# A conditioned ternary FFN on one core: c made three token groups ahead, in halves between the products of w1 and w3

## What is computed

```python
q_emb = relu(cond @ W3 + b3)                       # 128 x 256
v_sum = sum(x, axis=1, keepdims=True)              # x is 128 x 32 x 256
c = relu(((32 * x + v_sum) * q_emb[:, None, :]) @ W2 + b2)
w1q, w3q, w2q = ternary_quant(w1), ternary_quant(w3), ternary_quant(w2)
h1, h3 = c @ w1q.T, c @ w3q.T                      # 682 hidden columns
out = x + (silu(h1) * h3) @ w2q.T
# ternary_quant(w): s = mean(|w|); clip(round(w / s), -1, 1) * s
```

## Time and profile before

| | us |
|---|---|
| median of 3 runs | 182.1 |
| lowest and highest | 181.93, 182.63 |
| span of the profiled execution | 180.4 |
| PE busy in the span | 169.6 |
| DVE busy | 117.4 |
| ACT busy | 86.0 |
| POOL busy | 35.2 |

### The profile page before, as it was taken

The page is one execution under the profiler, slowest core; times in us unless marked ns, Lnnn a source line. Parts: engine busy times, 40 slices in busy tenths (PEclk is TensorE's granted clock), DMA queues, the critical chain, the costliest instruction groups (busy, mean ns, idle before and its releaser), DMA issues.

```text
span 180.4 us, 2908 instructions
## 1 busy us (share of the span) xinstructions
PE 169.6 (94%) x958; PEld 147.0 (81%) x958; DVE 117.4 (65%) x171; ACT 86.0 (48%) x142; POOL 35.2 (20%) x32
## 2 busy tenths in 40 slices
PE   6999899997379999999999999999999999999993
PEld 6788788885257898888889888888888988988893
DVE  0558999899993735674485565549357456744873
ACT  3135358857048744345463543555435443553640
POOL 4261677695925000000000000000000000000000
PEclk9999999999979999999999999999999999999999
DMA  4799734899000000030020003003000200300203
GB/s 94 244 336 360 231 116 124 280 359 290 0 0 5 0 0 0 0 116 0 0 90 26 0 0 116 0 0 116 0 0 19 97 0 0 116 0 0 89 31 116
DMA packets 14989, 15.21 MB, mean 84 GB/s; under 512 B 560, under 2 KB 14728, under 8 KB 14984
## 3 DMA queue, kind: packets, MB, share of 16 engines
q1 hardware_dynamic: 14976, 15.14, 25.7%
q10 hardware_dynamic: 8, 0.00, 0.0%
HBM read 10.94 MB, written 4.19 MB: 84 GB/s over the span
## 4 chain that ended last, share of the span: by engine, by line
PE 80%; DVE 10%; DMA 3%; issue 2%; ACT 2%; POOL 1%; SPq 0%; DVEq 0%; POOLq 0%
PE bank L482 46%; PE bank L512 23%; DVE w_t L607 5%; PE bank L403 5%; DMA w_sb<-in_L_ffn_w_dram 3%; DVE below L600 2%; PE bank L390 2%; PE bank L419 2%; DVE vsum L574 1%; POOL x L266 1%; ACT w_t L332 1%; PE bank L468 1%; PE bank L431 1%; ACT c_hi L318 1%; DVE y L579 0%
## 5 line engine op out<-in xcount | busy, mean ns | idle before, releaser
L482 PE MATMUL bank<-c_hi,T 128*128 (+3 forms) x176 | 69.9, 397 | 0.0
L482 PE MATMUL bank<-c_lo,T 128*128 (+3 forms) x176 | 69.7, 396 | 0.0
L355 ACT ACTIVATE y<-bank,checked 128x512 f32<-128x512 f32 (+1 forms) x48 | 33.0, 688 | 58.8 <-PE bank L482 58.8
L482 PEld LDWEIGHTS bank<-c_lo,T 128*128 128x128 f32 (+1 forms) x176 | 33.4, 190 | 6.2
L482 PEld LDWEIGHTS bank<-c_hi,T 128*128 128x128 f32 (+1 forms) x176 | 33.4, 190 | 6.2
L669 DVE TENSOR_TENSOR y<-y,bank 128x512 f32<-128x512 f32 x32 | 22.0, 686 | 22.1 <-PE bank L482 18.5
L512 PE MATMUL bank<-T,g_lo 128*128 128x256 f32 x160 | 32.7, 283 | 0.0
L512 PE MATMUL bank<-T,g_hi 128*128 128x256 f32 x160 | 32.5, 282 | 0.0
L403 PE MATMUL bank<-x,W_sb 128*128 128x256 f32 x128 | 29.9, 384 | 0.9 <-POOL x L266 0.9
L512 PEld LDWEIGHTS bank<-T,g_hi 128*128 128x128 f32 x160 | 27.1, 190 | 2.4
L669 DVE TENSOR_TENSOR x<-y,bank 128x512 f32<-128x512 f32 (+1 forms) x16 | 11.0, 688 | 26.5 <-ACT y L355 16.0
(11 more groups left out here) (61 smaller groups left out, 101.0 us busy)
## 6 DMA issues: line engine op xcount, KB each, us to landing
xo<-in_x_dram SPq DMA_DIRECT2D x1, 4096.0 KB, 16.9
out_dram<-xo SPq DMA_DIRECT2D x15, 256.0 KB, 2.2
xs<-in_x_dram SPq DMA_DIRECT2D x7, 512.0 KB, 3.9
w_sb<-in_L_ffn_w_dram SPq DMA_DIRECT2D x2, 640.0 KB
w_sb<-in_L_ffn_w_dram SPq DMA_DIRECT2D x1, 682.0 KB, 8.3
xs<-in_x_dram SPq DMA_DIRECT2D x2, 256.0 KB, 3.4
W_sb<-in_L_cond_W_dram SPq DMA_DIRECT2D x1, 256.0 KB, 5.2
out_dram<-xo SPq DMA_DIRECT2D x2, 128.0 KB, 2.0
```

The source lines that it names most:

```text
L355: nc.scalar.activation(silu[j % 2][r], h1[j % 3][r], ACT.Silu, scale=checked[r, 0:1]).then_inc(silu_done, 1)
L482: last = pe.matmul(dst[j % 3][0:w, :], T13[:, k, col:col + w], part[:, at(g), k, :], start=(i == 0), stop=(i == len(passes) - 1))
```

## The change

Only three groups (`AHEAD`), six halves, of c are made ahead. Half n of the other ten is made during the steps of the group three before its own: `half_at` places the transposes of its two halves behind the products of steps 0 and 2, and its multiplications by W2 behind those of steps 2 and 5. A half is now the unit of every engine's work on c: `relu(n)` is two ACT instructions of 256 columns, `hi_of_c` and `lo_of_c` one of 512, and `lo_of_c` is always POOL's. `ct` has four half buffers.

x is loaded once, straight into `xo`, from where PE transposes it; DMAs of x wait for nothing, and cond and W3 are loaded from ACT's queue. The rest rows of w1 and w3 are zeroed, so each of |w|'s sum, `below` and `w_t` is one instruction of 1536 columns, and all three sums of |w| are ACT's. `below` is formed with two operations, times -1 and greater than the limit, so `neg_limits` is gone. DVE instead of ACT copies w3's part of T13.

The h1 and h3 banks are two pairs in place of three; the banks set free hold `xT` (bank 6) and `z` (bank 7) during the layer. DVE does g and lo of the same step one behind the other. The group loops are written out.

```diff
-        h1 = [bank[:, 2 * s, :] for s in range(3)]
-        h3 = [bank[:, 2 * s + 1, :] for s in range(3)]
-        o = [bank[:, 6 + b, :].rearrange("p (t d) -> p t d", t=2) for b in range(TT // 2)]
...
+        h1 = [bank[:, 2 * s, :] for s in range(2)]
+        h3 = [bank[:, 2 * s + 1, :] for s in range(2)]
+        o = [bank[:, 4 + b, :].rearrange("p (t d) -> p t d", t=2) for b in range(TT // 2)]
+        o_last = bank[:, 6, 0:D]
...
+            g, j = m // STEPS, m % STEPS
+            return (g + AHEAD) * HALVES + at.index(j) if g + AHEAD < NG and j in at else None
...
+            for n in range(2):
+                sp.dma_start(xo[:, 1, n * HTT:(n + 1) * HTT], x_v[1, :, n * HTT:(n + 1) * HTT]
+                             ).then_inc(got_half[2 + n], 16)
+            sp.wait_ge(zeroed, 2)
+            sp.dma_start(w1_sb[:, 0:HC, :], w1[0:HC * P, :].rearrange("(j p) d -> p j d", p=P)).then_inc(got_w1, 16)
+            sp.dma_start(w1_sb[0:HR, HC, :], w1[HC * P:H, :]).then_inc(got_w1, 16)
+            sp.dma_start(xo[:, 2], x_v[2]).then_inc(got_group[0], 16)
+            sp.dma_start(w3_sb[:, 0:HC, :], w3[0:HC * P, :].rearrange("(j p) d -> p j d", p=P)).then_inc(got_w3, 16)
+            sp.dma_start(w3_sb[0:HR, HC, :], w3[HC * P:H, :]).then_inc(got_w3, 16)
             sp.dma_start(w2_sb[:], w2.rearrange("(c p) h -> p c h", p=P)).then_inc(got_w2, 16)
-            with sp.Fori(1, NG // 2 - 1) as i:
-                for u in range(2):
-                    sp.wait_ge(xT_done, (i * 2 + u + 1) * HALVES)
-                    sp.dma_start(xs[u][:], x_v[bass.ds(i * 2 + u + 2, 1)].rearrange("a p t d -> p (a t) d")
-                                 ).then_inc(got_xs[u], 16)
-            sp.dma_start(xo[:], x_v.rearrange("g p t d -> p g t d")).then_inc(got_xo, 16)
-            with sp.Fori(0, NG - 1) as g:
+            for g in range(3, NG):
+                sp.dma_start(xo[:, g], x_v[g]).then_inc(got_group[g - 2], 16)
...
+            scale_by_q(0)
+            scale_by_q(1)
+            for n in range(2, NH):
+                scale_by_q(n)
+                lo_of_c(n - 2)
+            lo_of_c(NH - 2)
+            lo_of_c(NH - 1)
...
+            relu(0)
+            hi_of_c(0)
+            abs_sum(0, w1_sb, w1_t, got_w1, 32)
+            relu(1)
+            hi_of_c(1)
+            relu(2)
+            hi_of_c(2)
+            abs_sum(1, w3_sb, w3_t, got_w3, 32)
+            relu(3)
+            hi_of_c(3)
+            abs_sum(2, w2_sb, w2_t, got_w2, 16)
+            relu(4)
+            hi_of_c(4)
+            copy_T13(0, T1_copied)
+            relu(5)
+            hi_of_c(5)
...
+            for m in range(NG * STEPS):
+                silu_step(m)
+                n = half_at(m - 1, (2, 5)) if m else None
+                if n is not None:
+                    relu(n)
+                hi_step(m)
+                if n is not None:
+                    hi_of_c(n)
+                if m == 0:
...
+            transpose_x(2)
+            project_c(0)
+            transpose_x(3)
+            project_c(1)
...
+            sum_partitions(0)
+            transpose_x(4)
+            project_c(2)
+            transpose_x(5)
+            project_c(3)
+            sum_partitions(1)
+            project_c(4)
+            transpose_w13(0, w1_t)
+            project_c(5)
+            transpose_w13(1, w3_t)
+            pe.wait_ge(T1_copied, 2)
+            sum_partitions(2)
...
-                pe.wait_ge(g_lo_done, g * STEPS + j + 1)
+            def h1_step(m):
+                j = m % STEPS
+                if j == 0:
+                    pe.wait_ge(c_lo_done, HALVES * (m // STEPS + 1))
+                if m >= 2:
+                    pe.wait_ge(g_done, m - 1)
+                hidden_product(m, h1, (j if j < HC else 2 * HC) * P, h1_done)
+            def h3_step(m):
+                hidden_product(m, h3, (HC + m % STEPS) * P, h3_done)
...
+            pe.wait_ge(y_done, EARLY)
+            pe.wait_ge(relu_done, DC * EARLY)
+            h1_step(0)
+            pe.wait_ge(limit_done, 3)
+            h1_step(1)
+            pe.wait_ge(T3_copied, 2)
+            h3_step(0)
+            transpose_w2()
+            h3_step(1)
+            LAST = (NG - 1) * STEPS
+            for m in range(NG * STEPS):
+                j = m % STEPS
+                if m >= 2:
+                    h1_step(m)
+                    if j < HC:
+                        h3_step(m)
+                n = half_at(m, (0, 2))
+                if n is not None:
+                    transpose_x(n)
+                n = half_at(m, (2, 5))
+                if n is not None:
+                    project_c(n)
+                ready = m - 2
+                if 0 <= ready < LAST and ready % STEPS != 0:
+                    if ready % STEPS == 1:
+                        output_step(ready - 1)
+                    output_step(ready)
...
+                nc.vector.tensor_scalar(below[:, 0:n], flat_weight(w_sb), -1.0, limits[:, k:k + 1], ALU.mult,
+                                        ALU.is_gt).then_inc(below_done, 1)
...
+            for n in range(4):
+                sum_sequence(n)
+                add_sum(n)
+            limit(0)
+            below_limit(0, w1_sb)
+            sum_sequence(4)
+            add_sum(4)
+            ternary(0, w1_sb, w1_t)
+            sum_sequence(5)
+            add_sum(5)
+            limit(1)
+            below_limit(1, w3_sb)
+            ternary(1, w3_sb, w3_t)
+            limit(2)
+            below_limit(2, w2_sb)
+            dve.wait_ge(wT_done, 2)
+            nc.vector.tensor_copy(T13[:, :, HC * P:2 * HC * P], w13_ps[1][:, :, 0:HC * P]).then_inc(T3_copied, 1)
+            nc.vector.tensor_copy(T13[:, :, 2 * HC * P + HR2:2 * HC * P + 2 * HR2],
+                                  w13_ps[1][:, :, HC * P:HC * P + HR2]).then_inc(T3_copied, 1)
+            nc.vector.tensor_scalar(scales[:], limits[:], 2.0, None, ALU.mult).then_inc(scale_step, 1)
             dve.wait_ge(scale_step, 1)
-            below_limit(w1_sb, 0)
-            sum_and_add(NG - 1, 1, halves=[0])
-            ternary(w1_sb, w1_t, 0)
-            scale_and_limits(1, slice(1, 3))
-            sum_and_add(NG - 1, 1, halves=[1])
+            nc.vector.reciprocal(inverse[:], scales[:]).then_inc(scale_step, 1)
             dve.wait_ge(scale_step, 2)
...
             nc.vector.scalar_tensor_tensor(out=checked[:], in0=inverse[:], scalar=0.0, in1=scales[:],
                                            op0=ALU.mult, op1=ALU.add).then_inc(scale_step, 1)
+            ternary(2, w2_sb, w2_t)
+            dve.wait_ge(scale_step, 3)
+            nc.vector.tensor_tensor(out_scale[:], checked[:, 1:2], checked[:, 2:3], ALU.mult).then_inc(scale_step, 1)
             dve.wait_ge(scale_step, 4)
...
-            g_step(0, 0)
-            dve.wait_ge(wT_done, 3)
-            nc.vector.tensor_copy(T2[:, 0:W2_HALF, :], w_ps[0][:, 0:W2_HALF * D].rearrange("p (j d) -> p j d", d=D)
-                                  ).then_inc(T2_copied, 1)
-            g_step(0, 1)
-            lo_step(0, 0)
-            g_step(0, 2)
-            lo_step(0, 1)
-            dve.wait_ge(got_xo, 16)
-            with dve.Fori(0, NG - 1) as g:
-                for j in range(STEPS):
-                    g_step(*later(g, j, 3))
-                    lo_step(*later(g, j, 2))
-                for b in range(TT // 2):
-                    residual(g, b, o[b], 2 * b, 2 * b + 2, g + 1)
-            for j in range(STEPS):
-                if j + 3 < STEPS:
-                    g_step(NG - 1, j + 3)
-                if j + 2 < STEPS:
-                    lo_step(NG - 1, j + 2)
+            for m in range(NG * STEPS):
+                g, j = m // STEPS, m % STEPS
+                g_step(m)
+                n = half_at(m, (0, 2))
+                if n is not None:
+                    sum_sequence(n)
+                if m == 0:
+                    dve.wait_ge(wT_done, 3)
+                    nc.vector.tensor_copy(T2[:, 0:W2_HALF, :],
+                                          w2_ps[0][:, 0:W2_HALF * D].rearrange("p (j d) -> p j d", d=D)
+                                          ).then_inc(T2_copied, 1)
+                lo_step(m)
+                if n is not None:
+                    add_sum(n)
+                if g and j == 1:
+                    for b in range(TT // 2):
+                        residual(g - 1, b, o[b], 2 * b, 2 * b + 2, g)
```

More of the change, by code:

```diff
@@ L296, in _ @@
             act.wait_ge(const_ready, 2)
[L297 removed]
+            nc.scalar.activation(warm[:], ident[:, 0:1], ACT.Silu)
             act.wait_ge(condT_done, 1)
@@ new lines, in sum_partitions, with transpose_w13 @@
+            def sum_partitions(k):
+                pe.wait_ge(abs_done, k + 1)
+                pe.matmul(sums_ps[k], ones[:], abs_sums[:, k:k + 1], start=True, stop=True).then_inc(sums_done, 1)
+            def transpose_w13(k, w_t):
+                pe.wait_ge(ternary_done, k + 1)
+                for c in range(DC):
```

(41 more changed lines are left out.)

456 lines of the change are left out of this document (160 added, 296 removed).

## The result

| | median, us | lowest to highest | runs |
|---|---|---|---|
| kernel before | 182.3 | 181.42 to 183.21 | 13 |
| changed kernel | 183.43 | 182.56 to 185.24 | 13 |

The ratio is 1.007, with a 95% interval of 1.0047 to 1.0093. The change makes the kernel about 1.2 us slower. The forecast was 181.8, no change; the time lies in the range and outside what the forecast called no change. The profiled execution took 185.24 us with a span of 183.4, so 1.8 us lie around the span. It is the slowest of the 13; the second one had a span of 181.2.

What follows compares the result with a forecast made beforehand. TensorE was taken as the bound: the layer's start plus the TensorE work behind it. Against the 180.4 us span, -24.7 + 21.65 + 2.7 = -0.35 gives 180.05; with 1.7 around it 181.8 us, range 179.0 to 184.9.

Steps and rivals of the forecast that it cites:

- no change: Outcome within half a per cent of 182.1 us, the kernel before: 181.2 to 183.0, chance 0.39.
- The start: End of group 0's second h3 product, claimed to move from 58.2 to 33.5 us, 24.7 us earlier.
- the walk: Adding up instruction times from c's first matmuls to group 0's second h3 product, with 2.1 us of VectorE waits for GpSimd.
- What is late behind it: TensorE's waits after the start, at halves 6 and 7 and in the last group: 2.7 us in all.
- c's work on TensorE: Matmuls and transposes of c, 4.33 us a group; five groups moved between the steps add 21.65 us.
- TensorE's stretch behind the start: TensorE's work after group 0's second h3 product, taken at the earlier profile's rates, plus 21.65 us for c.
- fetching instructions: Unrolled group loops make TensorE fetch more instructions: 0 to 0.5 us, taken as 0.
- A: Faster rival: GpSimd's delays of VectorE and waits at halves 6 and 7 close up; 177.9 at most, half 179.8; chance 0.28.
- B: Slower rival: VectorE's lo and GpSimd's c work block each other in groups 0 to 4; 1.5 to 5 us, middle 184.8; chance 0.12.
- C: Slower rival: `below` with two operations runs at w_t's rate, three cost 2.3 us more, 184.1; chance 0.09.
- D: Slower rival: the clock falls once in the ragged start, idle pieces between 28 and 38 us; 183.3; chance 0.12.

Runs made afterwards that it cites:

- ctl: The changed kernel without an edit, run again for a second profile; 183.42 us, ratio 1.0053 to the kernel before.
- d0: Changed kernel with 96 unused bytes behind T2, so c_hi lies 133 x 512 bytes behind T13; 182.17 us, ratio 0.9982 to the kernel before.
- before_d416: Kernel before with 416 unused bytes behind T2, so the distance from T13 to c_hi is 416 modulo 512; 183.66 us, ratio 1.0076.
- t3_act: Changed kernel with ScalarE instead of VectorE copying w3's part of T13; 181.96 us, ratio 0.9973 to the kernel before.
- t2_after: Changed kernel with VectorE's copy into T2 moved behind lo of step 0 and the addition of half 6; 182.55 us, ratio 1.0025.
- b_first: Changed kernel with the two small bias loads ahead of cond and W3 in ScalarE's queue; 182.94 us, ratio 1.0036 to the kernel before.
- combo_b: combo with W3's load put last in ScalarE's queue; 180.49 us, ratio 0.9886 to the kernel before.
- combo: Changed kernel with the edits of t3_act, t2_after and d0 together; 180.32 us, ratio 0.9881 to the kernel before.

## Why the prediction was wrong, step by step

**The start was right to 0.7 us, part of it by two errors that cancel.** The forecast put the end of the second h3 product of group 0 at 33.5 us. It was at 35.0 in the first profile and at 32.8 in ctl, and what lies between is the late bias load (1.3 us) and the slower matmuls behind it (1.0), which the forecast did not have: it took the start "nearly as before" and cost the move of cond and W3 to ScalarE's queue at nothing. Of the walk's terms one was too large: GpSimd cost VectorE 1.0 us there and not 2.1 (`below` 1.36 where 1.02 is undisturbed, the second w_t 2.48 against 1.81). Against that, the multiplications by W2 began at 9.47 us in ctl where the walk had 9.00, so the two misses of 1.1 and 0.5 leave the 0.7 us by which ctl is earlier than the forecast.

**What is late behind it** was right to 0.6 us: 1.07 and 0.41 at half 7 (forecast 1.2 and 0.65), and 0.6 in the last group (0.85).

**c's work on TensorE** was right: 1.73 us for eight multiplications and 0.44 for four transposes, twice each, are 4.34 a group (4.33).

**The step that failed is the one that carried most microseconds:** TensorE's stretch behind the start, which the prediction took over at the rates of the profile before, as 119.3 us plus the 21.65 of c; that is, it took the spacing of the product matmuls as unchanged. With the waits it forecast 143.65 us from the second h3 product to TensorE's last matmul. It took 145.1 us in the first profile and 145.0 in ctl, although the waits were 0.6 less: the term was too small by 2.0 us. 336 product matmuls at 3.8 ns more and 352 output matmuls at 0.3 are 1.4 of it; the other 0.6 are not placed (in ctl matmuls that restart behind a wait in the last group stand some 0.1 us further from the next one than the others, which is part of it). The prediction's only price for a slower stretch was 0 to 0.5 us for fetching instructions; it looked at the order of the instructions and not at the addresses of their operands, which the change also moves. That the spacing follows their distance is shown by d0 and before_d416; by what mechanism is not. Another 0.3 us stand behind the last matmul (3.25 us to the end of the span in place of 2.92), unexplained.

With the distance put back (d0) the median is 182.17, 0.4 us above the forecast of 181.8, and "no change" holds. So 96 unused bytes make the difference between the forecast and its miss.

**The rivals.** A (the layer's head not broken, 179.8) did not come by itself, but t3_act and t2_after, which close exactly the waits that it named, gained 1.5 and 0.9 (0.5 by the ratio). B (lo and c on one port) has its mechanism and not its price:

```profile
L568 DVE TENSOR_TENSOR g_lo<-gf,g_hi 128x512 fp32r<-128x512 f32 x40 | 33.6, 840 | 21.4 <-ACT g_hi L293 20.6
```

The mean of 684 ns in the earlier trace rows became 840, but no wait of TensorE follows from it in the middle groups. C is out: `below` takes 1.02 us for 1536 columns where it is undisturbed. D is out: no slice behind the start shows a lower clock. The fall that the kernel before has there is gone, and the forecast, which took the 4.29 us of the twelve matmuls as they were in one profile, counted it at its shorter length. The last group's own chain of g, cast and lo does end the program, at a cost of 0.4 us of idle TensorE ahead of its last output step.

**The sum for the first profile:** 180.05 forecast, +1.5 at the start, +1.5 behind it, +0.3 at the end give 183.35; the span is 183.4. For ctl: 180.05 - 0.7 + 1.4 + 0.3 = 181.05; the span is 181.1. That execution took 182.93 us: 181.05 and 1.85 around the span, where the forecast had 1.7. The median of the changed kernel is another 0.5 us higher; no execution near it was profiled, so that part is not placed.

## What to carry to other kernels

When the bound engine does the same instructions before and after, its rate is still a term of the sum and has to be priced: a change that adds, drops or reorders buffers moves the operands of its matmuls. Compare the time of one identical block (here sixteen product matmuls, 3.65 against 3.75 us) before looking for waits; if it differs, try a few unused bytes between the weights and the moving operand. And take a second profile before explaining a start: here a small load at the end of a queue that landed 1.3 us later, and eight matmuls that took 1.0 us longer, moved everything behind them by 2.3 us from one execution to the next. The same holds for the kernel before: its fall of the clock has two lengths, some 0.8 us of its time apart.

## What the runs showed of the hardware

- The spacing of fp32r matmuls of 512 columns changed with the distance in SBUF between what they load as weights and what they stream: 230 ns at 0 and 64 modulo 256 bytes, 232 at 128, 233.5 at 160; matmuls of 256 columns 119.1 to 119.7 ns, and 116.7 at 64. The Trainium skill, page "SBUF — State Buffer", section "Who interferes with whom", gives TensorE two independent read ports, for the moving operand and for the weights. From that alone one would not expect the distance to matter; these runs show that it does, by up to 1.7%, and not by what mechanism.
- Four loads on one queue at the start (two of 1 KB, one of 64 and one of 128): the last to be issued landed 2.9 to 5.1 us after its issue, and which one TensorE waited for changed with the order, but hardly the time at which it went on (b_first 9.86 us, combo_b 9.71, ctl 9.47).
- The first eight matmuls of c took 3.03 us behind a wait for the biases of 2.0 us, 2.01 behind 0.8 (ctl) and 1.5 (combo), and 2.49 behind 0.5 (d0), so it doesn't follow the wait. They were slow up to where the record of the granted clock begins: 12.8, 9.2, 9.6 and 10.2 us. What sets that point is open.
- The granted clock of the kernel before fell to half once, beside the 4.2 us in which TensorE waited for w_t up to 51 us: it was half from 51.7 to 55.0 us in one profile and from 49.7 to 56.4 in the other. Without that wait (the changed kernel) it did not fall before TensorE's last matmul.
